# Attention with post-norm and a gated FFN on one core: products with V of two steps issued together, over four buffers of exponentials

## What is computed

```
qkv  = einsum('bsd,ndh->bnsh', x, W_qkv)          # 16 heads of 16
q, k, v = split(qkv, 3)
attn = softmax(einsum('bnqh,bnkh->bnqk', q, k) * 0.25 + causal mask)
out  = einsum('bnqk,bnkh->bnqh', attn, v).reshape(B, -1, S)
x    = layernorm(x + einsum('bds,nhd->bsd', out, W_out))
x    = layernorm(x + ffn(x))      # 9 paths, one picked per row, then a norm
```

## The kernel before, in words

| step | 0 | 1 | 2 | 3 | 4 | 5 | 6 | 7 | 8 | 9 | 10 | 11 |
|---|---|---|---|---|---|---|---|---|---|---|---|---|
| mid | 0 | L710, 2, 3 | 5 | 6 | 7, 8 | 10 | 12 | 14 | 16 | 18 | 20 | 21 |
| end | 1 | 4 | | | 9 | 11 | 13 | 15 | 17 | 19 | | |

## Time and profile before

### The profile page before, as it was taken

How to read it: one execution, slowest core, us unless ns; L and a number is a source line. 1 busy time by engine, 2 the same in 40 slices (tenths; PEclk the granted TensorE clock), 3 DMA queues, 4 the chain that set the end, 5 groups by cost and what they waited for, 6 DMA issues and landing times. The chain is left out here.

```text
span 1690.4 us, 30405 instructions
## 1 busy us (share of the span) xinstructions
PE 1499.3 (89%) x9006; PEld 728.5 (43%) x9054; DVE 1092.9 (65%) x1735; ACT 961.0 (57%) x2085; POOL 438.9 (26%) x564
## 2 busy tenths in 40 slices
PE   5877988999998997997997997999995799999995
PEld 3544643333343343343333433333322465666664
DVE  3111238777776776775775776786730487888875
ACT  3444530666775765765665775676776554545442
POOL 5232430111112222312312312312313235222222
PEclk9888985999999998998998999999997899999998
DMA  3698765174777777678679579479534232111001
GB/s 118 215 189 226 239 180 58 23 81 55 89 107 94 86 113 105 86 98 125 76 85 149 68 86 155 61 90 159 62 92 84 93 70 76 50 50 50 26 26 37
DMA packets 348538, 165.98 MB, mean 98 GB/s; under 512 B 230813, under 2 KB 323816, under 8 KB 348392
## 3 DMA queue, kind: packets, MB, share of 16 engines
q1 hardware_dynamic: 348392, 164.12, 55.7%
HBM read 103.50 MB, written 59.77 MB: 97 GB/s over the span
## 5 line engine op out<-in xcount | busy, mean ns | idle before, releaser
L638 DVE TENSOR_REDUCE a_mx<-a_ps_m 128x1 f32<-128x640 f32 (+6 forms) x704 | 700.2, 1027 | 256.7 <-PE a_ps_m L706 252.5
L621 ACT ACTIVATE a_probs<-a_ps_s 128x512 f32<-128x512 f32 (+3 forms) x1536 | 641.7, 498 | 381.2 <-PE a_ps_s L753 376.7
L753 PE MATMUL a_ps_s<-s_qs,s_ks 99*128 99x512 bf16 (+3 forms) x1536 | 390.2, 333 | 48.3 <-issue 40.2
L701 PE MATMUL a_ps_m<-s_ks,s_qs 96*128 96x512 bf16 (+3 forms) x1536 | 396.9, 343 | 38.8 <-DVE a_mx L638 26.1
L579 POOL TENSOR_SCALAR_AFFINE_SELECT a_probs<-a_probs 128x512 f32<-128x512 f32 x256 | 163.1, 637 | 758.7 <-ACT a_probs L621 758.7
L729 PE MATMUL a_ps_o<-a_probs,s_vq 128*32 128x512 f32 (+3 forms) x3072 | 328.8, 500 | 1.9 <-POOL a_probs L579 1.9
L701 PEld LDWEIGHTS a_ps_m<-s_ks,s_qs 96*128 96x128 bf16 x1536 | 127.2, 100 | 294.6 <-DVE a_mx L638 146.3
L753 PEld LDWEIGHTS a_ps_s<-s_qs,s_ks 99*128 99x128 bf16 x1536 | 128.0, 98 | 216.0 <-ACT a_probs L621 102.8
L706 PE MATMUL a_ps_m<-s_mask,s_ident 128*128 128x128 bf16 (+1 forms) x832 | 192.8, 232 | 0.0
L225 DVE TENSOR_TENSOR p_rest<-p_ps_qk,p_parts 128x512 f32<-128x512 f32 x64 | 44.3, 692 | 174.2 <-ACT p_parts L250 174.2
L1280 PE MATMUL f_ps_h<-f_xm,f_w 128*128 128x512 f32 x320 | 147.3, 604 | 7.0 <-DVE f_xm L1128 7.0
(11 more groups left out here) (97 smaller groups left out, 1066.3 us busy)
## 6 DMA issues: line engine op xcount, KB each, us to landing
qk_parts<-p_parts SPq DMA_DIRECT2D x64, 384.0 KB, 2.9
s_qs<-qk_parts SPq DMA_DIRECT2D x192, 128.0 KB, 6.6
s_ks<-qk_parts SPq DMA_DIRECT2D x192, 128.0 KB, 6.8
p_x_rows<-in_L_attn_x_dram SPq DMA_DIRECT2D x16, 512.0 KB, 5.1
v_rows<-p_v_sb SPq DMA_DIRECT2D x16, 512.0 KB, 4.2
s_vq<-v_rows SPq DMA_DIRECT2D x64, 128.0 KB, 9.2
heads_out<-a_o_sb SPq DMA_DIRECT2D x128, 64.0 KB
f_x_in<-in_L_attn_x_dram SPq DMA_DIRECT2D x8, 1024.0 KB, 7.9
```

The source lines that it names most:

```text
L621: act.activation(probs[:, st % PB, h, 0:width], ps_s[:, n % BANKS, 0:width], ACT.Exp, scale=SCALE).then_inc(exps[h % 2], 1)
L638: dve.tensor_reduce(mx[:, e, heads[0]:heads[-1] + 1, qt], span(i), AX_X, ALU.max)\
L701: last = pe.matmul(out, qs[0:TROWS, j, h, q], ks[0:TROWS, j, h, s:s + wide], start=k == 0, stop=mask is None)
L753: pe.matmul(ps_s[:, n % BANKS, 0:width], ks[0:MROWS, j, h, kt * P:(kt + 1) * P], qs[0:MROWS, j, h, q0:q0 + width], start=True, stop=True)\
```

## The change

Of every two steps the products are issued together, behind the scores of the even step: at step `st` (even) those of `st - 2` and then those of `st - 1`; at step 0 those of steps 10 and 11 of the slot before. Odd steps issue none. `probs` has four buffers in place of three, since a step's exponentials are now read up to one step later. ACT's copies of `ps_o` come one step later, behind the exponentials of step 1 and of step 5. The number of matmuls, exponentials, units, masks, copies and DMAs is the same; `BANKS` and the two buffers of `ps_m` are as they were.

```diff
-        PB = 3
+        PB = 4
...
-                            if st == 0 and not (isinstance(t, int) and t == 0):
+                            if st == 1 and not (isinstance(t, int) and t == 0):
                                 keep_o(t - 1, (j - 1) % 2, 1, sent_before(*((b, j - 1) if j else (b - 1, QUADS - 1))))
-                            if st == CT:
+                            if st == CT + 1:
                                 keep_o(t, j % 2, 0, sent_before(b, j))
...
-                            if st >= 1:
-                                products(t, j, st - 1)
-                            elif before:
-                                products(t - 1, (j - 1) % QUADS, NST - 1)
+                            if st % 2 == 0 and (st or before):
+                                for k in (2, 1):
+                                    if st:
+                                        products(t, j, st - k)
+                                    else:
+                                        products(t - 1, (j - 1) % QUADS, NST - k)
...
-                products(SLOTS - 1, QUADS - 1, NST - 1)
+                for k in (2, 1):
+                    products(SLOTS - 1, QUADS - 1, NST - k)
```

## The result

| | before | changed |
|---|---|---|
| median of 4 runs, us | 1697.35 | 1728.34 |
| lowest to highest | 1694.81 to 1700.6 | 1726.29 to 1728.57 |
| span of the profiled execution | 1690.4 | 1726.6 |

The changed kernel is slower: ratio 1.018, 95% interval 1.016 to 1.020, 31 us. The forecast was 1734, range 1705 to 1756.

A forecast was written before the change was run, and what follows sets the result against it. PE was taken to set the slots' time. Per slot -1.30 + 1.10 + 1.57 - 0.28 = +1.09 us, thirty slots +32.7, then +2.4 + 3.0 - 1.7: +36.4, 1728.5 on the profiled scale, 1734 on the median's; range 1705 to 1756.

The forecast's parts named there:

- The seams: On PE, six pairs of products a slot each save 0.242 less 0.025 us of mode change: -1.30 us a slot.
- The rival in which a pair keeps its seam: Between a pair's two products the whole mode-change cost stays: 39 us more, 1773; chance 0.09, shared with a torn pair.
- The 1752: Total if each pair's second products wait for their weights, some 0.1 us a load: 18 us more.
- The split: Transpose to unit 5 stays 3.77 us; step 0's products move behind it, so PE waits longer: +1.10 us a slot.
- The new waits: From odd to even steps, PE waits for three banks and two unit buffers without products between: +1.57 us a slot.
- Small stops: PE's stops ahead of unit 9 (-0.16) and in step 1's scores (-0.12) go: -0.28 us a slot.
- A slot: Sum of the four per-slot terms, for each of thirty slots with units: +1.09 us.
- POOL: POOL is late for step 8's products in a few slots; these move back by a step: -1.7 us in all.
- The last two slots: Slots without units: two steps of 512 columns take 5.20 against 4.80 us, three such pairs in each: +2.4 us.
- The branches: At five loop branches step 10's products move behind PE's wait, 0.6 us each: +3.0 us.
- The rival in which the seams win: Faster, about 1687, if new waits for banks and units stay under 0.48 us a slot; chance 0.09.

The follow-up runs named there:

- the run with a score between: Changed kernel with head 3's score of every even step put between the two sets of products of each pair: 1759.8 us, ratio 1.038.
- The kernel with two pairs: Changed kernel with only steps 2 and 3 and steps 10 and 11 paired, copies where they stood before the change: 1687.1 us, ratio 0.993.

## Why the prediction was right, and where not

- **The seams**, -1.30: measured 6 x 0.242 = -1.45. The second products follow the first with no seam at all, 1.85 = 2 x 0.853 + 0.146, and the run with a score between puts the seams back one for one. The 0.025 of the earlier trace rows is not a seam: in a pair the four sets start at 704.31, 704.76, 705.19 and 705.62, so it is paid once, at the first set. The rival in which a pair keeps its seam, 1773, falls by this. The Trainium skill's rule (TensorE: Matmul & The Clock Gate, The mechanism), by which the second products would wait for their weights, isn't borne out: the four loads ahead of the third set, the first of the second products, stand at 704.76 to 704.89 in the trace, while the second set runs from 704.76 to 705.37, and the pair shows no gap. The 1752 that went by that rule falls too.
- **The split**, +1.10: the stretch is 3.77 in both kernels, and PE's idle time in it rose from 0.79 to 1.67 (1.9 was forecast), at unit 4 as well, as said. Taken back alone it gives 0.87 a slot, one seam less.
- **The new waits**, +1.57: measured 0.12 (3 to 4), 0.28 (5 to 6), 0.32 (head 3 behind the copy), 0.12 (7 to 8), 0.13 (unit 15), 0.28 (unit 19), 0.35 (unit 20), together 1.60. The third score of step 0 waits 0.10 besides, and head 3's of that step no longer its 0.09, where the prediction had both kernels alike. Two stops were taken away singly, and the slot fell by 0.33 and by 0.63 less a seam. The Trainium skill (Perfetto Trace Analysis, Optimization Strategy) says that a gap that repeats on the engine that should be full can mean too few buffers. The trace agrees as far as the waits go, for a bank and for a unit in turn, and moving units within a step only trades one for the other; that more banks or units would take them away is not shown.
- **Small stops**, -0.28: step 1's three scores take 0.49 for 0.62, and the 0.16 ahead of unit 9 is gone, -0.29.
- **A slot**, +1.09: these add up to +0.97, and from transpose to transpose it is +1.05; 0.08 has no place. That is the step that carried the forecast, and it held.
- **POOL**, -1.7: weight loads still wait for POOL, more often, but for 0.2 at most where it was 0.9. PE's own wait for it, 1.2 us in that window, is gone; the -1.7 itself is not measured apart:

```profile
PEld a_ps_o L729 <- POOL a_probs L579: 3.9, 16, 0.2
```

- **The last two slots**, +2.4: +4.9. The mechanism was right and the clock's fall in one pair of each not foreseen.
- **The branches**: this step failed. "At five branches step 10's products (0.6 us) stand right ahead of the branch now and can lie beside PE's wait for it; they will be behind it. [...] I take 0.6 [...]: +3.0." PE's work ahead of the stop doesn't add to it. The stop's end is set from elsewhere: PE reached it 0.2 to 0.8 later and left it 1.0 earlier on average. The seven fourth slots came out 9.3 under what their growth by 1.04 each would give, in place of the +3.0; the six stops are 8.4 us shorter, and the rest wasn't taken apart.
- **Not foreseen**: the third slots (+6.8), of which 5.2 in the six with the reciprocal, since the 0.8 of the earlier trace rows was read from a slot without it, and 1.5 in the first batch's; and some 3 us in the first slots and slot 0. Much of both is the fall of the clock, for which the sum had no term. These, the last two slots' 2.5 and the branch nearly cancel: on the profiled execution's scale the sum gave 1728.5, and it took 1728.35. That the total is this near is luck; that a slot is, isn't. The 6 us between 1734 and 1728.3 are the step from that scale to the median's: the executions of the kernel before spread over 6 us, and its profiled one lay low.

The rival in which the seams win fell on its own condition: the new waits are 1.60 in a slot and had to be under 0.48. The kernel with two pairs, which is faster than the one before, is not that rival: it has few new waits, and it also leaves the split covered.

## What to carry to other kernels

Before work is moved to save a change of mode between matmuls, list for each place it leaves what it covered there: a stretch that another engine sets keeps its length, and the moved work comes on top of it. Here six seams of 0.242 were worth less than one uncovered split of 1.10 and seven small waits; pairing only where nothing was covered gave a kernel 0.7% faster than before. And look apart at stops whose end is set from elsewhere. At the branch they were 19.2 us in all in the kernel with the longest slots (31.90), 31.8 in the changed one (30.78), 40.2 before (29.73) and 48.8 with two pairs (29.07), so that they took back part of what the slots gained or lost. It is no strict order: with steps 0 and 1 single (29.91) they were 46.5.

## What was not expected of the hardware

- Between two products in the same four column strips there is no seam: 1.85 us for 16 records of 512 columns. Between whole-array matmuls and these it is 0.096 to go in and 0.146 to come out.
- The stop at the loop's branch ends 1.6 to 2.7 us behind the landing of an instruction packet, at 70 of 70 branches that go back; the four sends took 14.07 us to issue behind the loads and 4.25 ahead of them, and the six stops together were longer for it. That the stop waits for instructions is likely from this and not shown.
- The granted clock fell to the 1.2 GHz level for 3.4 us behind a stop of 1.61 us in mid-slot, but at four of six such stops, and in a pair of each of the last slots with stops of 0.59 us ahead, which the kernel before has without a fall. The kernels with two pairs have no fall outside the branches. In other versions such falls stood elsewhere, which is one reason why totals moved less evenly than slots; what sets them here isn't settled.
